# Last attention without f32 copies of queries and keys; first attention's entry in another order

## The reference

```
x = x + tanh(g_xattn[L]) * attention_L(layernorm(x), ctx)      # L = 0..3
x = x + tanh(g_ffn[L])   * ffn_L(layernorm(x))
```

```
q = (input @ Wq + bq) ; kv = encoded_features @ Wkv + bkv       # attention 3
scores = einsum('bhqd,bhkd->bhqk', q, k) / sqrt(16)
attn = softmax(scores, axis=2)
out = einsum('bhqk,bhkd->bhqd', attn, v) @ Wo + bo
```

## Time and profile before

| | us |
|---|---|
| median of 3 runs | 1953.98 (1951.7 to 1955.2) |
| the profiled execution | 1958.57 |
| its span, first to last instruction | 1956.8 |
| PE busy | 1601.6 (82%) |
| DVE busy | 1103.2 (56%) |
| ACT busy | 831.6 (42%) |
| POOL busy | 296.5 (15%) |

### The profile page before, as it was taken

How to read it: one execution, slowest core, us unless ns; L and a number is a source line. 1 busy time by engine, 2 the same in 40 slices (tenths; PEclk the granted TensorE clock), 3 DMA queues, 4 the chain that set the end, 5 groups by cost and what they waited for, 6 DMA issues and landing times.

```text
span 1956.8 us, 29283 instructions
## 1 busy us (share of the span) xinstructions
PE 1601.6 (82%) x10374; PEld 1213.9 (62%) x10375; DVE 1103.2 (56%) x2538; ACT 831.6 (42%) x1851; POOL 296.5 (15%) x361
## 2 busy tenths in 40 slices
PE   5899872993888773578878999999879873999997
PEld 3566662882555542455544778787645452999997
DVE  5666628314899997866644353535469966222221
ACT  3455530323776642255545522212379941222221
POOL 1101100531121100111100000000102202233332
PEclk7899985997899986789989999999989975999999
DMA  7355234226553511544415000000456625522221
GB/s 160 50 83 77 45 127 171 43 38 126 119 111 84 102 36 46 76 63 69 67 23 239 2 1 1 1 1 17 71 70 107 105 85 197 159 38 35 34 38 27
DMA packets 86462, 144.08 MB, mean 74 GB/s; under 512 B 14299, under 2 KB 69987, under 8 KB 83139
## 3 DMA queue, kind: packets, MB, share of 16 engines
q1 hardware_dynamic: 66562, 102.86, 22.5%
q0 software_dynamic: 19776, 39.60, 12.8%
HBM read 75.50 MB, written 27.66 MB: 53 GB/s over the span
## 4 chain that ended last, share of the span: by engine, by line
PE 55%; DVE 24%; ACT 7%; issue 6%; DMA 5%; SPq 1%; POOL 0%; POOLq 0%; DVEq 0%; ACTq 0%
PE ps L1373 12%; PE ps L1481 7%; PE ps L1492 7%; PE ps L1342 4%; DVE probs L2218 3%; DMA Qpack<-QP 3%; PE ps L875 2%; PE ps L1254 2%; ACT pT L1618 2%; PE ps L1018 2%; PE ps L965 2%; PE ps L1263 2%; DVE hpart L2199 2%; PE ps L904 2%; PE ps L956 2%
## 5 line engine op out<-in xcount | busy, mean ns | idle before, releaser
L347 POOL DMA_DIRECT2D Kpack<-KP x192 | 101.3, 536 | 969.8 <-PE ps L1373 384.3
L1613 ACT ACTIVATE pT<-ps 128x512 f32<-128x512 f32 x256 | 151.7, 606 | 192.1 <-PE ps L959 98.7
L956 PE MATMUL ps<-Qpack,Kpack 99*128 99x256 bf16 (+1 forms) x768 | 166.5, 283 | 27.4 <-ACT pT L1618 11.6
L1481 PEld LDWEIGHTS ps<-xgT,XNT 128*128 128x128 f32 x1248 | 146.5, 193 | 1.9
L1481 PE MATMUL ps<-xgT,XNT 128*128 128x128 f32 x1248 | 146.7, 276 | 0.0
L1492 PE MATMUL ps<-w,mid 128*128 x624 | 141.0, 379 | 0.0
L925 PE MATMUL ps<-Kpack,Qpack 97*128 97x256 bf16 x512 | 103.6, 289 | 39.8 <-DMA Qpack<-QP 10.9
L1887 ACT ACTIVATE mid<-ps 128x512 f32<-128x512 f32 x78 | 42.4, 595 | 201.8 <-PE ps L1481 196.6
L1618 ACT ACTIVATE pT<-ps,nmax 128x256 f32<-128x256 f32 x256 | 121.0, 551 | 14.5 <-DVE nmax L2131 14.4
L2119 DVE CUSTOM_DVE_ANT_0 Vb<-ps,mask_bf 128x256 bf16<-128x256 f32 x256 | 95.0, 419 | 52.4 <-PE ps L925 52.3
L1492 PEld LDWEIGHTS ps<-w,mid 128*128 128x128 f32 x624 | 115.6, 190 | 14.1
(11 more groups left out here) (312 smaller groups left out, 3302.0 us busy)
## 6 DMA issues: line engine op xcount, KB each, us to landing
Kpack<-KP POOLq DMA_DIRECT2D x192, 128.0 KB, 5.0
Qpack<-QP SPq DMA_DIRECT2D x192, 128.0 KB, 6.0
w<-in_w SPq DMA_DIRECT2D x16, 1024.0 KB, 6.0
ctxT<-in_ctxT SPq DMA_DIRECT2D x32, 256.0 KB, 7.4
h_rows<-in_h SPq DMA_DIRECT2D x16, 512.0 KB, 6.4
h<-h_rows SPq DMA_DIRECT2D x2, 4096.0 KB, 22.2
wd<-in_wd SPq DMA_DIRECT2D x4, 1536.0 KB, 14.4
xn_rows<-xn SPq DMA_DIRECT2D x16, 256.0 KB, 2.4
```

The source lines that it names most:

```text
L347: eng.dma_start(Kpack[j][DH * k:DH * (k + 1)].rearrange("d (e f) t -> d e (f t)", f=HALF), KP[par][:, part]).then_inc(done, 16)
L956: mm = pe.matmul(A[h % ring][:, t], Kpack[par][0:rows, h, t * P:(t + 1) * P], Qpack[par][0:rows, h], start=True, stop=L != 0)
L1481: mm = pe.matmul(bank[:, f % 4 * P:(f % 4 + 1) * P], w1_tile[k % 2][:, c, f * P:(f + 1) * P], xgT3[k % 2][:, c], start=c == 0, stop=c == K ...
L1613: act.activation(pT[h % 8][:], A[h % 2][:], ACT.Exp).then_inc(s["exp_done"], 1)
```

## The change

Two parts, and what they need.

1. `DIRECT = (3,)`: in attention 3 ACT writes only the bf16 plane 0. DVE's rest reads the PSUM bank itself, adds the bias and subtracts plane 0, in two instructions of 128x256 instead of one of 128x512. Since DVE now reads the bank last, PE's waits before reusing it are for `k_r1` and `q_r1`, raised by the rests, in place of `k_evac` and `q_evac`. The scale 1/4 moves from ACT's copies into Wq, which DVE multiplies in place in `biases`; PE's query products wait for that.
2. Attention 0's entry: `HEAD[0] = 2`. X arrives in pieces of 4, 6 and 6 tiles (before 2, 7 and 7), the first behind the context of batch 0 and Wk in SP's queue; the context of batch 1 and the two further pieces come directly behind the query bias. Statistics, deviations and normalising of pairs 0 and 1 come first, then the splits of pair 0, then the statistics of the other 12 tiles, then the splits of pair 1. PE turns pair 1 and projects its keys and queries directly after pair 0's. The deviations of the 12 tiles and the normalising of pairs 2 and 3 stand among the row maxima of batch 0 (after heads 1, 3 and 5), as in attention 2. The tanh of the gates comes after the second square root. The six DMAs of the fixed rows are issued by POOL ahead of its first key pack, with a semaphore of their own (`pack_rows0`).

```diff
+DIRECT = (3,)
-HEAD = {0: 1, 1: 1, 2: 2, 3: 2}
+HEAD = {0: 2, 1: 1, 2: 2, 3: 2}
-X_PIECES = (0, 2, 9, NT)
+X_PIECES = {0: (0, 4, 10, NT), 1: (0, 2, 9, NT)}
...
+        def fixed_rows(eng, L):
+            for par in range(PACK_RING):
+                for rows, src in ((Kpack[par][MASK_ROW:MAX_ROW + 2], ones_bf[0:3]),
+                                  (Qpack[par][MASK_ROW:MASK_ROW + 1], (zeros_bf if L == 0 else ones_bf)[0:1])):
+                    eng.dma_start(rows.rearrange("r h (a c) -> r (h a) c", c=P),
+                                  src.unsqueeze(1).to_broadcast([src.shape[0], H * S // P, P])).then_inc(s["pack_rows0" if L == 0 else "pack_rows"], 16)
...
                 for w, name in ((wk[:], "wk"), (bk[:], "bk"), (wq[:], "wq"), (bq[:], "bq")):
                     sp.dma_start(w, a[f"{name}{L}"]).then_inc(s["qk_loaded"], 16)
+                    if L == 0 and name == "wk":
+                        next(x_pieces)
                 if L == 0:
+                    load_ctx(1, 1)
+                    next(x_pieces)
                     sp.dma_start(gb[:, 0:4], a["g_xattn"].partition_broadcast(P)).then_inc(s["gates_loaded"], 16)
                     sp.dma_start(gb[:, 4:8], a["g_ffn"].partition_broadcast(P)).then_inc(s["gates_loaded"], 16)
-                    next(x_pieces)
...
+                if L == 0:
+                    pool.wait_ge(s["rt_const"], 1)
+                    fixed_rows(pool, L)
...
+                k_read, q_read = (s["k_r1"], s["q_r1"]) if L in DIRECT else (s["k_evac"], s["q_evac"])
...
-                            wait(pe, s["k_evac"], 8 * i + b)
+                            wait(pe, k_read, 8 * i + b)
...
+                        if L in DIRECT:
+                            pe.wait_ge(s["bias_ready"], 2 * i + 1)
...
                         elif not keys and b > 0:
-                            pe.wait_ge(s["q_evac"], 8 * i + min(b + 2, B))
+                            pe.wait_ge(q_read, 8 * i + min(b + 2, B))
...
                 if L == 0:
                     pe.wait_ge(s["qk_loaded"], qk_total(i))
                     proj_k(0, 0, 0)
-                if HEAD[L] == 1:
+                    turn_pair(n, 0)
+                    proj_q(0)
+                    turn_pair(n, 1)
+                    proj_k(1, 1, 0)
+                    proj_q(1)
+                elif L == 1:
...
                     for f in range(HALF):
-                        act.activation(kf[:, f], keys_in(L, b)[:, f], ACT.Identity, bias=bk[:, f:f + 1])
+                        if L not in DIRECT:
+                            act.activation(kf[:, f], keys_in(L, b)[:, f], ACT.Identity, bias=bk[:, f:f + 1])
                         e = act.activation(KP[par][:, 0, f], keys_in(L, b)[:, f], ACT.Identity, bias=bk[:, f:f + 1])
...
+                if L == 0:
+                    deviations(chains[n], slice(0, 2 * ST))
+                    split_k(0, 0, 0)
+                    pair_out(n, 0)
+                    middle_k(0, 0)
+                    split_q(0, 0, 0)
+                    pair_out(n, 1)
+                    middle_q(0, 0)
+                    split_k(1, 1, 0)
+                    middle_k(1, 1)
+                    split_q(1, 1, 0)
+                    middle_q(1, 1)
+                    deviations(chains[n] + 1, slice(2 * ST, NT))
+                    act.wait_ge(s["gates_loaded"], 32)
+                    act.activation(tg[:], gb[:], ACT.Tanh).then_inc(s["tg_ready"], 1)
...
+                if L in DIRECT:
+                    dve.tensor_scalar(wq[:], wq[:], INV_SQRT, None, ALU.mult)
...
-                    dve.tensor_tensor(qr[:], qf[:], QP[par][:, 0], ALU.subtract).then_inc(s["q_r1"], 1)
+                    if L in DIRECT:
+                        for f in range(HALF):
+                            e = dve.scalar_tensor_tensor(qr[:, f], queries_in(L, b)[:, f], bq4[:, f:f + 1], QP[par][:, 0, f], ALU.add, ALU.subtract)
+                    else:
+                        e = dve.tensor_tensor(qr[:], qf[:], QP[par][:, 0], ALU.subtract)
+                    e.then_inc(s["q_r1"], 1)
...
+                if L == 0:
+                    constants()
+                    dve.wait_ge(s["x_load0"], 16)
+                    for t in range(2 * ST):
+                        statistics(t)
+                    deviations(n, chains[n], slice(0, 2 * ST))
+                    normed_pair(n, 0)
+                    normed_pair(n, 1)
+                    biases(0)
+                    rest_k(0, 0)
+                    low_k(0, 0)
+                    rest_q(0, 0)
+                    low_q(0, 0)
+                    dve.wait_ge(s["x_load1"], 32)
+                    for t in range(2 * ST, NT):
+                        statistics(t)
+                    rest_k(1, 1)
+                    masks()
+                    low_k(1, 1)
+                    rest_q(1, 1)
+                    low_q(1, 1)
+                    dve.wait_ge(s["mask_ready"], 1)
...
-                        if h == 1 and L == 2:
+                        if h == 1:
                             deviations(n, chains[n] + 1, slice(2 * ST, NT))
```

More of the change, by code:

```diff
@@ L439, in _, with load_x @@
                 sp.sem_inc(xn_out[j], SENT0)
-            def load_x(rows):
+            def load_x(rows, L):
                 for k in range(3):
-                    tiles = slice(X_PIECES[k], X_PIECES[k + 1])
+                    tiles = slice(X_PIECES[L][k], X_PIECES[L][k + 1])
                     sp.dma_start(X[:, tiles], rows.rearrange("(t p) c -> p t c", p=P)[:, tiles]).then_inc(s[f"x_load{min(k, 1)}"], 16)
@@ L475, in loads @@
                     sp.dma_start(mask_u8[:, 1], a["mask_kq"]).then_inc(s["mask_loaded"], 16)
-                load_ctx(1, 1)
+                if L != 0:
+                    load_ctx(1, 1)
                 for w, name in ((bv, "bv"), (bo, "bo")):
@@ L479, in loads @@
                 sp.dma_start(wo[:, 0:HALF] if L in SOFTMAX_KEYS else wo[:], a[f"wo{L}"]).then_inc(s["w_loaded"], 16)
-                if L in SOFTMAX_KEYS:
+                if L == 2:
                     sp.wait_ge(s["rt_const"], 1)
-                    for par in range(PACK_RING):
-                        for rows, src in ((Kpack[par][MASK_ROW:MAX_ROW + 2], ones_bf[0:3]),
-                                          (Qpack[par][MASK_ROW:MASK_ROW + 1], (zeros_bf if L == 0 else ones_bf)[0:1])):
-                            sp.dma_start(rows.rearrange("r h (a c) -> r (h a) c", c=P),
-                                         src.unsqueeze(1).to_broadcast([src.shape[0], H * S // P, P])).then_inc(s["pack_rows"], 16)
+                    fixed_rows(sp, L)
                 if L == 2:
@@ L586, in ffn @@
                     sp.wait_ge(s["f0_scatter"], 16 * SL0 * E0)
-                    for _ in load_x(x_rows[0:T]):
+                    for _ in load_x(x_rows[0:T], 1):
                         pass
@@ L618, in ffn @@
                         sp.sem_inc(s["f3_loaded"], 1)
-            x_pieces = load_x(a["x"])
-            next(x_pieces)
+            x_pieces = load_x(a["x"], 0)
             for n, (kind, L) in enumerate(stages):
@@ L1078, in attention @@
                 elif L == 3:
[L1079 to L1080 removed]
+                    pe.wait_ge(q_read, 8 * i + 2)
+                    pe.wait_ge(k_read, 8 * i + 2)
                 if not keys:
@@ L1569, in split_k @@
                         act.wait_ge(pack_k[j], keys_packed(i, j, (b - 2) // pack_ring(L) + 1))
-                    wait(act, s["k_r1"], g)
+                    if L not in DIRECT:
+                        wait(act, s["k_r1"], g)
                     for f in range(HALF):
-                        act.activation(kf[:, f], keys_in(L, b)[:, f], ACT.Identity, bias=bk[:, f:f + 1])
+                        if L not in DIRECT:
+                            act.activation(kf[:, f], keys_in(L, b)[:, f], ACT.Identity, bias=bk[:, f:f + 1])
                         e = act.activation(KP[par][:, 0, f], keys_in(L, b)[:, f], ACT.Identity, bias=bk[:, f:f + 1])
@@ L1581, in split_q @@
                         act.wait_ge(pack[j], packed(i, j, (b - 2) // pack_ring(L) + 1))
-                    wait(act, s["q_r1"], g)
+                    if L not in DIRECT:
+                        wait(act, s["q_r1"], g)
                     for f in range(HALF):
-                        act.activation(qf[:, f], queries_in(L, b)[:, f], ACT.Identity, bias=bq4[:, f:f + 1], scale=INV_SQRT)
-                        e = act.activation(QP[par][:, 0, f], queries_in(L, b)[:, f], ACT.Identity, bias=bq4[:, f:f + 1], scale=INV_SQRT)
+                        if L in DIRECT:
+                            e = act.activation(QP[par][:, 0, f], queries_in(L, b)[:, f], ACT.Identity, bias=bq4[:, f:f + 1])
+                        else:
+                            act.activation(qf[:, f], queries_in(L, b)[:, f], ACT.Identity, bias=bq4[:, f:f + 1], scale=INV_SQRT)
+                            e = act.activation(QP[par][:, 0, f], queries_in(L, b)[:, f], ACT.Identity, bias=bq4[:, f:f + 1], scale=INV_SQRT)
```

(19 more changed lines are left out.)

35 lines of the change are left out of this document (10 added, 25 removed).

## The result

The changed kernel takes 1943.3 us (median of 8 runs, 1939.65 to 1948.19) where the kernel before takes 1954.07 beside it (8 runs). The ratio on record is 0.9934, 95% interval 0.9916 to 0.9952: about 12.9 us less (the two medians differ by 10.8). The forecast was 1941.3, between 1934 and 1950, 12.7 us less.

What follows compares the result with a forecast made beforehand. It took the entry as a serial chain with no engine full, and the last attention as led by ACT, PE and DVE close; 1954.0 - 12.7 (entry 6.0, last attention 6.7) = 1941.3 us, range 1934 to 1950.

Steps and rivals of the forecast that it cites:

- The last attention: -6.7 forecast: Last attention: dropping ACT's f32 copies saves 6.7 us in sum, bounds -8.7 and +2.
- five slots of -1.2: Last attention, one slot per batch: batches 1 to 5 each get 1.2 us shorter from 19.73, together -6.0 us.
- slot 0: Last attention's first slot: the keys' copy gives 0.7 us; the queries' copy gives 0.7, which the rest takes back.
- PE now waits for the rest: 1519.6, no later: Last attention's slot: PE's value product waits for DVE's rest, not ACT's copy, and still starts no later than 1519.54.
- ACT's waits for DVE's maxima: Last attention's slots: ACT waited 11.5 us on DVE's maxima; a sign of the forecast was that ACT's waits on DVE grow.
- DVE takes the gain: Rival, last attention: DVE's extra 1.6 us over four slots keeps slots at 19.7, total 1948; chance 0.12.
- The clock falls in the slots: Rival, last attention: PE drops to 1.2 GHz, +14 us per slot, one slot 1955, two 1969; chance 0.04.
- The entry: -6.0 forecast: First attention's entry: first row maximum 6.7 us earlier, 0.7 given back, carried to the end; bounds -7.5 and -2.4.
- I take +0.5 (bounds 0 and +1.4): Entry's start: 256 KB more ahead of the query bias costs 1.4 us, one issue less gives 0.4; taken as +0.5.
- Landing in 4.5, at most 9.6: Entry: batch 0's query pack, issued by 24.9, lands 4.5 us later at 29.4, or at most 9.6 us later.
- the pack decides the entry: Rival, entry: the query pack lands at 34.5, first maximum waits, entry gives only -2.4, total 1945; chance 0.08.
- What comes back: 0.7: Entry, batch 0's maxima: deviations and pair 2's normalising fit DVE's idle time; pair 3's normalising costs 0.7 us.

Runs made afterwards that it cites:

- experiment 9: Changed kernel plus unused TensorE matmuls: 24 in the entry, 10 behind the first attention, 14 ahead of attention 2, 20 ahead of and 10 behind the last; 1950.89 us.
- experiment 5: The changed kernel once more, unaltered, run beside the last attention's part alone; 1943.14 us, ratio 0.9922.
- experiment 12: Changed kernel plus unused TensorE matmuls: 24 in the entry, 10 behind the first attention's last output product, 10 behind the last attention's; 1936.33 us, ratio 0.9889.
- experiment 1: Kernel before with only the new entry of the first attention, last attention as it was; 1949.99 us, ratio 0.996.
- experiment 4: Changed kernel with the loads of context 2 and 3 in the first attention issued behind both query packs; 1947.49 us, ratio 0.9937.
- experiment 7: Changed kernel plus 10 unused TensorE matmuls behind the last attention's last output product; 1937.41 us, ratio 0.9907.
- experiment 10: Changed kernel with the last attention's keys split through the f32 copy again, queries still directly; 1943.79 us, one run.
- experiment 11: Changed kernel with the packs' fixed rows issued by the sync engine again, behind the first attention's loads, not by GpSimd; 1939.36 us, one run.
- experiment 2: Kernel before with only the last attention's part (no f32 copies), entry as it was; 1945.94 us, ratio 0.9928.
- experiment 6: Kernel before with only the last attention's part, run again beside the changed kernel; 1946.82 us, ratio 0.9949.
- experiment 8: Changed kernel plus unused TensorE matmuls: 10 behind the last attention's last output product, 24 in the first attention's entry before the first scores; 1933.93 us, ratio 0.9883.
- experiment 3: Changed kernel plus 48 unused TensorE matmuls in the entry between pair 1's queries and the first scores; 1953.01 us, ratio 0.9986.

## Why the prediction came out as it did

The total was right: 1941.3 against 1943.3. That is in part luck: the traces give about 3 us more than forecast for the last attention and about 3 less for the first, and the two cancel.

**The last attention: -6.7 forecast, about -9.5 measured.** From the end of feed-forward 2 to its own end it takes 188.8 and 188.9 us in the two profiles without this part, and 178.2 to 181.3 in the ten with all of it (without experiment 9, which stood longer ahead of it). The mechanism and its size per slot were right: five slots of -1.2 (19.70 to 18.50), each rest 0.88, the query copy's wait nearly gone. Three things lay outside the five slots in the profiled pair, 3.6 us against 0.7 forecast. From the end of the stop to the first output copy it is 41.59 before and 40.39 after, -1.2, of which 0.7 was forecast for slot 0. The stop itself went from 12.24 to 11.33; it was 12.0 and 12.2 in the two profiles without the change and 10.8 to 11.9 in those with it. Nothing here tells why. From the sixth output copy to the end it is 36.51 before and 35.00 after. This last one is no fixed gain: with the changed code it was 33.7 (experiment 5) and 36.45 us (experiment 12) in other executions.

One step was wrong inside a right slot: "PE now waits for the rest: 1519.6, no later". It waits 0.98 us where it waited 0.70, up to 1.6 at the edges, over the 1 us that was to have shown the forecast wrong. It did no harm, because DVE and not PE was the next bound. The forecast also had ACT's waits for DVE's maxima grow; they did not (4.0 and 4.1 us in four slots).

**"DVE takes the gain"** was half a rival. DVE is the bound now, at 98%, but 7.1 of its 7.7 idle us in four slots before were waits for ACT, as the prediction argued against it; of the 7.3 us that the rival rests on, 0.2 lie in these slots. **"The clock falls in the slots"** didn't come about: 1.00 through all of them.

**The entry: -6.0 forecast, -2.7 in the mean at the end of the stage.** Seven profiled executions of kernels with the new entry and nothing filled in there (after, experiments 1, 4, 5, 7, 10, 11) stand against three with the old one (before, experiments 2, 6). Means, in us:

| | old entry | new entry | difference | forecast |
|---|---|---|---|---|
| first projection begins | 7.34 | 8.56 | +1.2 | +0.5 |
| first row maximum | 35.80 | 31.72 | -4.1 | -6.7 |
| from there to the turn of the maxima | 16.7 | 18.7 | +2.0 | +0.7 |
| end of the first attention | 270.8 | 268.1 | -2.7 | -6.0 |

The ends of the first attention lie between 265.6 and 270.7 in the seven and between 269.8 and 271.7 in the three, so the 2.7 is good to some 2 us. At the end of feed-forward 2, with the same code between, the same profiles are 4.7 us apart in the mean (1409.9 and 1405.2), and by the ratios the entry is worth 7.8 us in experiment 1 and 5.3 between experiments 5 and 6. That it gains is clear; its size is known only as 3 to 8 us. What fell short is the start of the stage, where the steps can be read one by one.

The steps that failed:

- "I take +0.5 (bounds 0 and +1.4)". Measured +1.2. The prediction's own working gives 1.4 less 0.4, 1.0, and then takes half of it without a reason.
- The time it was counted from. The profiled execution of before ran pair 0's queries at half clock (3.77 us, 2.0 in the two others with the old entry) and had its first maximum at 36.87, where those had 35.28 and 35.25. That is 1.1 us over the mean of the three, chance of one profile.
- "Landing in 4.5, at most 9.6". The last query pack takes 7.96 us after, and 4.40 to 9.20 in the seven profiles; all seven have the scores waiting for it. The rival "the pack decides the entry" had the mechanism right. Its 34.5 was too late, since the issues came earlier than forecast (19.9 instead of 21.1), projections having kept the full clock. In the changed kernel's second profile (experiment 5) the first maximum came at 33.20, past the 33 that the prediction named as a sign of being wrong. The entry's bound of -2.4 is also mis-added: a landing at 34.5 puts the first maximum at 35.3 by its own 0.8, and the 0.7 that comes back is left out, which makes -0.9.
- "What comes back: 0.7". The new entry has PE waiting from 20.3 to 31.2, and behind this it runs at 1.2 GHz, so the value projection and batch 2's keys take 3.62 us each and the maxima wait for them. The prediction took the projections' durations from before, where only the value projection was slow, and never asked what 11 idle us would do to the clock. It asked this only of the last attention. The phase's length goes with these two products: 19.2 to 19.5 us where both take 3.62 (after, experiments 4, 7 and 11), 18.0 with only the keys slow (12), 17.1 with only the value projection slow (10), 16.0 with neither (8). The old entry has only the value projection slow and takes 16.5 (2 and 6). At like clocks the new phase is thus 0.6 longer, which is the forecast's 0.7; the rest is the clock of batch 2's keys.

**The rest of the profiled 16.2 us** is the router: 5.8. A forecast can't have it, but a reader of two profiles can be fooled by it.

## What to carry to other kernels

Removing the copies that lead a balanced loop pays most of their length (1.2 of 1.43 us a slot here) until the next engine is full; work the slot out on paper, engine by engine: here it came out to 0.1 us. Where a change opens an idle stretch ahead of f32 matmuls, count those at half clock, and see whether matmuls that nothing uses fit in. They cost nothing where PE waits longer than they take, the difference where the data come earlier (3 us in the entry of experiments 9 and 12), and more than their length where PE stands for another reason (experiment 9). Before a stage is explained from two profiles, look whether stages that the change doesn't touch also differ.

## What was not expected of the hardware

- The same code behind the same 4.72 us stop ran at either clock, six executions at the lower and four at the higher, worth 5.8 us, whatever the kernel.
- One matmul of 128x256 f32 stands as two instructions and takes 0.435 us at full clock (20.88 us for 96 of them, experiment 3).
- PE stood 3.30 us between two like matmuls without a wait (experiment 9), and 10.1 us ahead of them with none of their data missing. In all 14 profiled executions PE goes on from this stop 1.7 to 2.0 us behind the last packet of its stretch on the instruction queue.
